# Layer 3's edge sweep: four groups' logits in one go, the scatter in two column halves, the leaky relu split between ScalarE and VectorE

## Chip, cores, metric

The kernel runs on 1 core of a Trainium2 chip. A time is the device time of one execution in microseconds (us). Names of engines: PE is TensorE, DVE VectorE, ACT ScalarE, POOL GpSimd, SP SyncE.

## What is computed

A chain of four graph layers over 6250 nodes and 100,000 edges (sorted by destination, padded to 106,496), features of 128 numbers, all in fp32, each layer with a residual and a layer norm ahead. The change touches the third, a GATv2 attention layer with H = 8 heads of O = 16:

```python
xl = (x @ W_l + b_l).reshape(-1, H, O)
xr = (x @ W_r + b_r).reshape(-1, H, O)
ee = (edge_attr @ W_e).reshape(-1, H, O)
m = jax.nn.leaky_relu(xl[src] + xr[dst] + ee, 0.2)
logits = jnp.einsum('eho,ho->eh', m, att)
lmax = jax.ops.segment_max(logits, dst, num_segments=N)
exl = jnp.exp(logits - lmax[dst])
denom = jax.ops.segment_sum(exl, dst, num_segments=N)
msg = xl[src] * (exl / (denom[dst] + 1e-16))[:, :, None]
out = jax.ops.segment_sum(msg, dst, num_segments=N).reshape(-1, H * O) + b_att
h = layer_norm(x + out)
h = layer_norm(h + gelu(h @ W1 + b1) @ W2 + b2)
```

Layers 1 and 2 are a sum and a mean over edges, layer 4 two smaller attention convolutions.

## The kernel before

The program is a row of phases: setup, `term_sweep` (layer 1), `norm1_phase`, `sum_sweep` (layer 2), `soft_sweep(2)` (layer 3), `ffn_phase`, `soft_sweep(3)` and `soft_sweep(4)` (layer 4). A sweep goes over G = 208 groups of GE = 512 edges, four tiles of 128 edges (TPG) each. Four consecutive groups are a batch (BATCH = 4).

Every engine has its own hand-written program, a function `step(t)` that is called for t = 0 to G + 7; what an engine does for group g in step t is set by `t.back(k)`, that is g = t - k. `sweep16` unrolls 16 steps into one turn of a loop. Engines meet only at semaphores, and each runs its own list in order. `wait_past(eng, sem, g, n, add)` waits for n * g + add counts.

`soft_sweep(2)`, called soft2 below, with lines of the kernel before:

- GpSimd gathers the 512 source rows of a group, four indirect DMAs (L1792), into one of 16 slots of `rows`; a slot is free when `message` of 16 groups earlier is done.
- TensorE, step t: `edge_terms(t)` transposes the four row tiles (L1867) and computes W_e times edge attributes plus destination rows times one-hot columns (L1873, L1874) into one PSUM bank, `term_bank`. `scatter(t-7)` (L1908) multiplies a one-hot (128 edges x 64 nodes of a window) with the message (128 edges x 136: 128 features and 8 weights), four tiles into one bank. `head_logits(t-1)` (L1881) multiplies `att8[:, j]` with `z`; each of a batch's four groups adds its 8 heads into its own rows of 32 lanes. `flip_window(t-7)` (L1930, L1931) transposes the window.
- Once in four steps: the carry matmul (L1956), the init matmul (L1940), four lane transposes (L1963) and the factor matmuls (L1969, L1970).
- ScalarE: copy of the transposed rows into `z` (L1829), the message's weight columns (L1824), the window (L1834), per batch the lanes (L1850), exponentials (L1838, L1840) and weights (L1818).
- VectorE: the leaky relu of t-1 in place in `z` (L2075), the addition of window t-8 into the sums in SBUF (L2009 to L2018), the message t-7 (L2066), the edge sum (L2094); per batch two scans over 512 columns for the running maximum (L2028, L2034), the carry (L2041, L2044), the shift of the lanes (L2050 to L2060) and the factors (L2080, L2081).
- SyncE issues the loads: attributes, one-hot columns, destination rows, one-hots (L1765, which waits for the scatter three groups earlier), and per batch `starts` and `cont`, the masks of the scans.

## Time and profile before

| | us |
|---|---|
| median of 3 runs | 7552.22 |
| lowest, highest | 7548.44, 7554.60 |
| span of the profiled execution | 5796.6 |
| median less span | 1755.6 |
| soft2, first to last start of TensorE's row transposes | 2290.1 to 3371.0 |

The profiled execution's own time was not kept. The span goes from the first to the last instruction in the profile; the runs' times are longer by a part that no row shows. An engine's busy time in a stretch is the sum of its instructions there without overlaps; matmuls are pipelined, so the length of one is longer than its share of the engine: the distance from one start to the next tells what it costs. A row of the timeline merges equal neighbours (x4), and behind it, in brackets, stands how long the engine was idle before it and what ended that.

### The profile page before, as it was taken

Reading aid. Unit: us, or ns where it says so; the run is one execution under the profiler, and the core shown is the slowest. Engines: PE = TensorE matmul, PEld = TensorE weight load, DVE = VectorE, ACT = ScalarE, POOL = GpSimd, SP = SyncE. Lnnn points to the kernel's source line nnn. Section 1 sums busy time; section 2 is a strip of 40 time slices with the busy share of each in tenths; the row PEclk is TensorE's granted clock in tenths of the full one; section 3 lists DMA queues with packets and bytes.
Section 4 is the critical chain, followed back from the end, with each engine's and each line's share of the span. In section 5 each row is a group of like instructions: output and inputs, shape, how many; then the busy total and the mean of one; then the engine's idle time right before and its main releaser. Section 6 shows DMA issues by size and latency. Waiting matters only on the chain. (4 is left out here: it accounts for less than half of the span.)

```text
span 5796.6 us, 89863 instructions
## 1 busy us (share of the span) xinstructions
PE 4596.1 (79%) x21959; PEld 3153.3 (54%) x21959; DVE 2702.8 (47%) x8105; ACT 1216.6 (21%) x3182; POOL 3988.9 (69%) x4207
## 2 busy tenths in 40 slices
PE   5888888657777776999999977687777758887887
PEld 4777777535556564444444433455555535555555
DVE  4222222321111113677777766555555545555555
ACT  2111111221211211222222258111111111111111
POOL 6777777457777775777777700777777747777775
PEclk9999999975555555999999989666666666666665
DMA  5333333244444443555555510455555534444443
GB/s 151 106 105 105 105 104 104 74 150 106 112 114 107 118 114 90 160 165 165 165 165 164 166 38 24 109 114 114 113 114 115 113 77 107 111 109 110 109 111 78
DMA packets 559823, 663.58 MB, mean 114 GB/s; under 512 B 196431, under 2 KB 390909, under 8 KB 558717
## 3 DMA queue, kind: packets, MB, share of 16 engines
q1 hardware_dynamic: 424909, 382.99, 22.2%
q0 software_dynamic: 134640, 277.80, 21.1%
q14 instruction: 207, 1.70, 0.1%
q8 instruction: 67, 1.10, 0.1%
HBM read 580.95 MB, written 86.19 MB: 115 GB/s over the span
## 5 line engine op out<-in xcount | busy, mean ns | idle before, releaser
L1792 POOL DMA_INDIRECT soft_rows<-table,sources x2496 | 2388.6, 957 | 1128.2 <-issue 737.7
L1422 POOL DMA_INDIRECT sum_rows<-table,sources x832 | 785.7, 944 | 343.9 <-issue 249.6
L1088 POOL DMA_INDIRECT term_rows<-table,sources x832 | 791.4, 951 | 289.4 <-issue 289.4
L1923 PE MATMUL psum<-soft_onehot,soft_message 128*128 128x64 f32 x3328 | 647.6, 358 | 107.1 <-DVE soft_message L2066 105.0
L1923 PEld LDWEIGHTS psum<-soft_onehot,soft_message 128*128 128x128 f32 x3328 | 586.1, 266 | 188.0 <-issue 181.8
L1119 PE MATMUL psum<-term_onehot,term_term 128*128 128x64 f32 x1664 | 403.9, 425 | 188.5 <-DVE sums L1171 176.6
L1464 PE MATMUL psum<-sum_onehot,sum_rows 128*128 128x64 f32 x1664 | 360.4, 391 | 222.7 <-DMA sum_rows<-table,sources 218.4
L1119 PEld LDWEIGHTS psum<-term_onehot,term_term 128*128 128x128 f32 x1664 | 370.7, 328 | 242.1 <-issue 242.0
L1165 DVE TENSOR_TENSOR term_term<-psum,term_rows 128x512 f32<-128x512 f32 x208 | 143.9, 692 | 753.0 <-issue 349.0
L1464 PEld LDWEIGHTS psum<-sum_onehot,sum_rows 128*128 128x128 f32 x1664 | 343.5, 304 | 278.0 <-issue 273.8
L1919 PEld LDWEIGHTS psum<-soft_onehot,soft_weights 128*4 128x4 f32 (+1 forms) x3328 | 284.9, 109 | 305.9 <-issue 293.0
L1109 PE MATMUL psum<-L_We,term_attrs 64*128 64x128 f32 x1664 | 430.5, 438 | 8.4 <-DMA term_attrs<-in_ea64T 8.4
L2066 DVE TENSOR_TENSOR soft_message<-soft_rows,psum 128x512 f32<-128x512 f32 x624 | 418.0, 670 | 2.9 <-issue 2.9
L1892 PE MATMUL psum<-soft_onehotT,soft_dst_cols 128*16 128x512 f32 (+1 forms) x416 | 375.4, 1004 | 49.4 <-DMA soft_dst_cols<-adst 49.4
L1109 PEld LDWEIGHTS psum<-L_We,term_attrs 64*128 64x128 f32 x1664 | 370.0, 325 | 56.4 <-issue 28.6
L1919 PE MATMUL psum<-soft_onehot,soft_weights 128*4 128x64 f32 (+1 forms) x3328 | 358.5, 272 | 12.4 <-DVE weight_sums L2011 0.9
L1097 ACT ACTIVATE term_term<-term_term 128x512 f32<-128x512 f32 x208 | 130.9, 630 | 913.0 <-DVE term_term L1165 913.0
L2016 DVE TENSOR_TENSOR sums<-sums,psum 128x64 f32 x624 | 136.7, 219 | 380.3 <-PE psum L1923 320.5
L1898 PE MATMUL psum<-ident,soft_src_cols 128*16 128x128 f32 (+1 forms) x832 | 173.5, 379 | 175.9 <-ACT soft_src_cols L1806 174.5
L1441 ACT ACTIVATE sum_flat<-psum 64x512 f32<-64x512 f32 x208 | 122.7, 590 | 830.9 <-PE psum L1454 826.4
L1503 DVE TENSOR_TENSOR sums<-sums,psum 128x64 f32 x208 | 46.2, 222 | 530.0 <-PE psum L1465 526.8
L1908 PEld LDWEIGHTS psum<-soft_message,soft_onehot 128*64 128x64 f32 x1664 | 188.1, 139 | 139.6 <-issue 138.8
(277 smaller groups left out, 6619.9 us busy)
## 6 DMA issues: line engine op xcount, KB each, us to landing
soft_onehotT<-onehotsT SPq DMA_DIRECT2D x312, 256.0 KB
soft_onehot<-onehots SPq DMA_DIRECT2D x624, 128.0 KB, 2.1
soft_attrs<-in_ea128T SPq DMA_DIRECT2D x208, 256.0 KB
soft_rows<-table,sources POOLq DMA_INDIRECT x2496
term_attrs<-in_ea64T SPq DMA_DIRECT2D x208, 128.0 KB, 2.8
onehots<-term_onehot SPq DMA_DIRECT2D x208, 128.0 KB
sum_onehot<-onehots SPq DMA_DIRECT2D x208, 128.0 KB, 2.7
onehotsT<-sum_flat SPq DMA_DIRECT2D x208, 128.0 KB
```

The source lines that it names most:

```text
L1088: pool.indirect_dma_start(rows[:, k, t, :], None, io.table0[0:NCH * CN], bass.IndirectOffsetOnAxis(sb.sources[:, g * TPG + t:g * TPG + t + ...
L1109: last = pe.matmul(term_bank[g.slot(4)][:, piece(b)], attrs[:, g.slot(AHEAD), piece(b)], sb.L0_We, start=True, stop=True)
L1119: last = pe.matmul(window[q], term[:, g.slot(4), b, :], onehot[:, g.slot(8), b], start=b == 0, stop=b == TPG - 1)
L1422: pool.indirect_dma_start(rows[:, k, t, :], None, io.table1[0:NCH * CN], bass.IndirectOffsetOnAxis(sb.sources[:, g * TPG + t:g * TPG + t + ...
L1464: pe.matmul(window[q], rows[:, g.slot(AROUND), b, 0:D], onehot[:, k, b], start=b == 0, stop=b == TPG - 1)
L1792: pool.indirect_dma_start(rows[:, k, t, :], None, table[0:NCH * CN], bass.IndirectOffsetOnAxis(sb.sources[:, g * TPG + t:g * TPG + t + 1], ...
L1892: pe.matmul(lane_bank[g.half()], dst_cols[:, j // 2], onehotT[:, pair(g)], start=j == 1, stop=False).then_inc(s.edge_term, 2)
L1898: last = pe.matmul(lane_bank[g.half()][:, piece(b)], src_cols[:, b], sb.ident, start=False, stop=b == TPG - 1)
L1908: last = pe.matmul(window_bank, onehot[:, k, b], message[:, g.slot(2), b, :], start=b == 0, stop=b == TPG - 1)
L1919: pe.matmul(bank[0:H, P:P + W], weights[:, q, b, j::BATCH], onehot[:, k, b], start=b == 0, stop=b == TPG - 1)
L1923: last = pe.matmul(bank[:, 0:W], message[:, g.slot(4), b, :], onehot[:, k, b], start=b == 0, stop=b == TPG - 1)
L2066: v.tensor_tensor(message[:, g.slot(2 if full else 4), :, 0:D].rearrange("p t (h c) -> p t h c", h=H), rows[:, g.slot(AROUND), :, 0:D].rea ...
```

## The change

soft2 gets a function of its own, `gatv2_sweep`; soft3 and soft4 keep `soft_sweep`, from which its branches for layer 3 are cut.

- **Logits.** `z` has four slots instead of two. `head_logits` runs once in four steps, for the whole batch, four groups back: four matmuls, each with the same `att_cols` (128 x 32, of which 8 columns hold the attention vector) and its own slot of `z`, into partitions 0 to 31, 32 to 63, 64 to 95 and 96 to 127 of `lane_bank`. Lanes, `starts` and `cont` so have 128 partitions, 32 a group with 8 in use; there is one `lane_bank`, and SyncE loads `starts` and `cont` in four pieces each.
- **Scatter.** Tiles 0 and 2 add into partitions 0 to 63 of the window bank, tiles 1 and 3 into 64 to 127. The window is copied with 128 partitions, and `flip_window` follows the scatter at once; it multiplies with `fold` (two 64 x 64 identities, one over the other), which turns the window and adds the halves.
- **Leaky relu.** VectorE adds the transposed rows, which ScalarE copied to `raw`, in place in PSUM (`term_bank`, now two banks). ScalarE writes a fifth of that into `z`. VectorE takes the maximum of both.
- The lane transposes become matmuls with `quad_pick`, which leaves out the empty lanes; the other small operands are laid out for 128 partitions. On VectorE the window's addition comes ahead of the leaky relu, and the backward scan behind the edge sum. `onehotT` has two slots of two groups instead of four.

```diff
-                    wait_past(pe, s.z, g, 1, 0)
+                    wait_past(pe, s.leaky, g, 1, -1)
...
                 def head_logits(g):
-                    j = g.slot(BATCH)
-                    pe.wait_ge(s.leaky, g.times(1, 1))
-                    if j == 0 and g.back(2 * BATCH).exists():
-                        pe.wait_ge(s.shifted, g.back(2 * BATCH).uses(BATCH))
-                    pe.matmul(lane_bank[g.half()], sb.att8[:, j], z[:, g.slot(2)], start=j == 0, stop=j == BATCH - 1).then_inc(s.logits, 1)
+                    pe.wait_ge(s.leaky, g.times(1, BATCH))
+                    if g.back(BATCH).exists():
+                        pe.wait_ge(s.factor_log, g.back(BATCH).uses(BATCH))
+                    settle(pe)
+                    for j in range(BATCH):
+                        last = pe.matmul(lane_bank[j * QUAD:(j + 1) * QUAD], sb.att_cols, z[:, j], start=True, stop=True)
+                    last.then_inc(s.logits, 1)
...
                     for b in range(TPG):
-                        last = pe.matmul(window_bank, onehot[:, k, b], message[:, g.slot(2), b, :], start=b == 0, stop=b == TPG - 1)
+                        last = pe.matmul(window_bank[b % 2 * W:b % 2 * W + W], onehot[:, k, b], message[:, g.slot(2), b, :], start=b < 2, stop=b >= TPG - 2)
...
                 def flip_window(g):
                     pe.wait_ge(s.window_copied, g.times(1, 1))
                     wait_past(pe, s.order, g, ORDER, 0)
                     settle(pe)
-                    pe.transpose(window_T[0][:, 0:W], window[:, 0:D], sb.ident[0:W, 0:W])
-                    pe.transpose(window_T[0][0:H, P:P + W], window[:, D:D + H], sb.ident[0:W, 0:W]).then_inc(s.window_T, 1)
+                    pe.matmul(window_T[:, 0:W], window[:, 0:D], fold, start=True, stop=True)
+                    pe.matmul(window_T[0:H, P:P + W], window[:, D:D + H], fold, start=True, stop=True).then_inc(s.window_T, 1)
...
-                            last = pe.transpose(weights_bank[:, b * L:(b + 1) * L], lanes[:, piece(b)], sb.ident[0:L, 0:L])
+                            last = pe.matmul(weights_bank[:, b * L:(b + 1) * L], lanes[:, piece(b)], sb.quad_pick, start=True, stop=True)
...
+                        act.activation(z[:, g.slot(BATCH)], term_bank[g.slot(2)], ACT.Copy, scale=0.2).then_inc(s.fifth, 1)
...
-                        act.activation(z[:, g.slot(2)], rows_bank, ACT.Copy).then_inc(s.rows_out, 1)
+                        act.activation(raw[:, g.slot(2)], rows_bank, ACT.Copy).then_inc(s.rows_out, 1)
...
-                        v.scalar_tensor_tensor(z[:, g.slot(2)], z[:, g.slot(2)], 0.2, z[:, g.slot(2)], ALU.mult, ALU.max).then_inc(s.leaky, 1)
+                    v.tensor_tensor(z[:, g.slot(BATCH)], term_bank[g.slot(2)], z[:, g.slot(BATCH)], ALU.max).then_inc(s.leaky, 1)
...
-                        v.tensor_tensor(z[:, g.slot(2)], term_bank, z[:, g.slot(2)], ALU.add).then_inc(s.z, 1)
+                    v.tensor_tensor(term_bank[g.slot(2)], term_bank[g.slot(2)], raw[:, g.slot(2)], ALU.add).then_inc(s.z, 1)
```

TensorE, the step that holds the init and lane matmuls, before (`psum<-` names what a matmul reads, then the output's shape):

```order
L1867 MATMUL psum<-ident,soft_rows 128x128 x4
L1873 MATMUL psum<-soft_attrs,L_We 128x512
L1874 MATMUL psum<-soft_onehotT,soft_dst_rows 128x512
L1940 MATMUL psum<-ones,soft_shift 32x1
L1908 MATMUL psum<-soft_message,soft_onehot 64x136 x4
L1881 MATMUL psum<-soft_z,att 32x512
L225 REGISTER_ALU
L1930 MATMUL psum<-ident,soft_window 128x64
L1931 MATMUL psum<-ident,soft_window 8x64
L1963 MATMUL psum<-ident,soft_lanes 128x32 x4
```

and now, the same step:

```order
L1827 MATMUL psum<-ident,soft_rows 128x128 x4
L1833 MATMUL psum<-soft_attrs,L_We 128x512
L1834 MATMUL psum<-soft_onehotT,rel_group 128x512
L1871 MATMUL psum<-ones,soft_shift 128x1
L1852 MATMUL psum<-soft_message,soft_onehot 64x136 x4
L225 REGISTER_ALU
L1859 MATMUL psum<-soft_fold,soft_window 128x64
L1860 MATMUL psum<-soft_fold,soft_window 8x64
L1889 MATMUL psum<-quad_pick,soft_lanes 128x32 x4
```

The logits are gone from between scatter and flip. They stand ahead of the scatter in one step of four:

```order
L1833 MATMUL psum<-soft_attrs,L_We 128x512
L1834 MATMUL psum<-soft_onehotT,rel_group 128x512
L1842 MATMUL psum<-soft_z,att_cols 32x512 x4
L1852 MATMUL psum<-soft_message,soft_onehot 64x136 x4
L225 REGISTER_ALU
L1859 MATMUL psum<-soft_fold,soft_window 128x64
```

There four matmuls run in a row where each step had one. VectorE, the step with the forward scan, before, from the window's addition on:

```order
L2018 TENSOR_TENSOR weight_sums<-weight_sums,psum 8x64
L2066 TENSOR_TENSOR soft_message<-soft_rows,psum 128x4x128
L2023 REGISTER_ALU
L2027 REGISTER_ALU
L2028 SCALAR_TENSOR_TENSOR psum<-soft_starts,psum 32x512
L2032 TENSOR_SCALAR soft_fend<-lane_mask,psum 32x4
L2034 SCALAR_TENSOR_TENSOR psum<-soft_starts,psum 32x512
L2092 REGISTER_ALU
L2094 TENSOR_TENSOR soft_z<-psum,soft_z 128x512
```

and now:

```order
L1938 TENSOR_TENSOR weight_sums<-weight_sums,psum 8x64
L1990 TENSOR_TENSOR soft_z<-psum,soft_z 128x512
L1983 TENSOR_TENSOR soft_message<-soft_rows,psum 128x4x128
L1942 REGISTER_ALU
L1943 REGISTER_ALU
L1944 SCALAR_TENSOR_TENSOR psum<-soft_starts,psum 128x512
L1948 TENSOR_SCALAR soft_fend<-quad_mask,psum 128x4
L1993 REGISTER_ALU
L1995 TENSOR_TENSOR psum<-psum,soft_raw 128x512
L1952 SCALAR_TENSOR_TENSOR psum<-soft_starts,psum 128x512
```

The leaky relu (L1990, the maximum) has come between the addition and the message, and the edge sum (L1995) ahead of the backward scan (L1952).

## Rows read from the trace of the kernel before

**Rows 1.** The page: span and instructions.

```profile
span 5796.6 us, 89863 instructions
```

**Rows 2.** Busy time by stretch: stretch, us, each engine, clock, DMA share, GB/s.

```profile
0.00:28.00 28.00, 5.55 (x20) 3.58 (x20) 14.11 (x81) 13.38 (x35) 23.24 (x47) 1.00 0.94 275
2320.00:2330.00 10.00, 8.48 (x24) 3.31 (x22) 3.81 (x9) 4.03 (x8) 7.56 (x9) 0.67 0.40 117
2371.00:3327.00 956.00, 933.82 (x4214) 437.03 (x4214) 690.39 (x1785) 278.55 (x776) 729.27 (x744) 1.00 0.56 165
3385.00:3407.00 22.00, 13.24 (x58) 9.85 (x56) 6.81 (x29) 3.26 (x13) 0.00 (x0) 0.50 0.02 6
```

**Rows 3.** Groups of soft2, 2300 to 3390: busy, mean ns | idle before, releasers.

```profile
L1792 POOL DMA_INDIRECT soft_rows<-table,sources x818 | 801.3, 980 | 249.4 <-issue 245.5 <-DVE soft_message L2066 4.0
...
L2075 DVE SCALAR_TENSOR_TENSOR soft_z<-soft_z 128x512 f32<-128x512 f32 x207 | 142.3, 688 | 31.8 <-issue 26.9
...
L1829 ACT ACTIVATE soft_z<-psum 128x512 f32<-128x512 f32 x206 | 123.0, 597 | 193.7 <-PE psum L1867 188.2
...
L2034 DVE TENSOR_TENSOR_SCAN psum<-soft_starts,psum 32x512 f32<-32x512 f32 x52 | 63.3, 1217 | 1.8
```

**Rows 4.** The gathers of soft3, 3700 to 4500, from the same view.

```profile
L1792 POOL DMA_INDIRECT soft_rows<-table,sources x641 | 605.5, 945 | 195.4 <-issue 191.7 <-DVE soft_message L2066 3.7
```

**Rows 5.** Line 1867, the row transposes: durations, first and last start.

```profile
L1867 PE MATMUL psum<-ident,soft_rows x832: 272/273/477, 2290.1 to 3371.0; 128*128 128x128 f32 x167
```

**Rows 6.** Timeline of TensorE over four steps: start, us, what.

```profile
2896.38 0.65 PE L1867 MATMUL psum<-ident,soft_rows 128*128 128x128 f32 x4
2896.87 1.02 PE L1873 MATMUL psum<-soft_attrs,L_We 128*128 128x512 f32 x2
2897.83 1.12 PE L1874 MATMUL psum<-soft_onehotT,soft_dst_rows 64*128 64x512 f32 x2
2898.88 1.14 PE L1908 MATMUL psum<-soft_message,soft_onehot 128*64 128x136 f32 x8
2899.95 1.05 PE L1881 MATMUL psum<-soft_z,att 128*32 128x512 f32 x2
2900.93 0.27 PE L1930 MATMUL psum<-ident,soft_window 64*128 64x64 f32 x1
...
2901.18 0.66 PE L1867 MATMUL psum<-ident,soft_rows 128*128 128x128 f32 x4
...
2911.31 0.40 PE L1963 MATMUL psum<-ident,soft_lanes 32*128 32x32 f32 x4 [0.17 <-ACT soft_lanes L1838]
2911.73 0.35 PE L1969 MATMUL psum<-soft_factors,lane_expand 32*128 32x4 f32 x2
2912.01 0.19 PE L1970 MATMUL psum<-soft_factors,lane_head 32*8 32x4 f32 x2
...
2916.94 0.33 PE L1867 MATMUL psum<-ident,soft_rows 128*128 128x128 f32 x1
```

**Rows 7.** Timeline of the drain of soft2: window copy, flip.

```profile
3381.27 0.28 ACT L1834 ACTIVATE soft_window<-psum 64x136 f32<-64x136 f32 x1 [1.76 <-PE psum L1908]
...
3381.69 0.24 PE L1930 MATMUL psum<-ident,soft_window 64*128 64x64 f32 x1 [0.46 <-ACT soft_window L1834]
```

**Rows 8.** Timeline of VectorE: the shift of the lanes.

```profile
2909.05 0.74 DVE L2055 SCALAR_TENSOR_TENSOR psum<-soft_cont,soft_init,psum 32x512 f32<-32x512 f32 x1
2909.83 0.68 DVE L2057 TENSOR_TENSOR soft_lanes<-soft_lanes,psum 32x512 f32<-32x512 f32 x1
```

**Rows 9.** Timeline: a leaky relu, the gather inside it, the next addition.

```profile
2894.91 0.69 DVE L2075 SCALAR_TENSOR_TENSOR soft_z<-soft_z 128x512 f32<-128x512 f32 x1
2895.02 1.40 POOL L1792 DMA_INDIRECT soft_rows<-table,sources  x1 [0.30 <-issue]
...
2896.28 0.21 DVE L2009 TENSOR_SCALAR sums<-sums,soft_factor_of  x1 [0.68 <-issue]
```

**Rows 10.** SyncE's waits in soft2: us in total, times, longest.

```profile
SPq L1765 <- PE psum L1908: 521.1, 203, 6.2
```

More of the change, by code:

```diff
@@ L1659, in soft_sweep @@
+    spread = {3: sb.lane_expand4, 4: sb.ones}[layer]
     mask, heads = sb.lane_mask[0:L], sb.lane_head[0:L, 0:H]
     AHEAD = 4
-    DST = AHEAD if full else BATCH
     phase = f"soft{layer}"
-    FIRST = AROUND if full else 4 * AROUND
-    LAST = G + LAG if full else STEPS * (NCH - 1 + BEHIND) + 14
-    names = ("order cleared starts_in cont_in rows_T rows_out edge_term z leaky src_out logits lanes_out running backward fend carry_psum carry shift init_psum init maxima "
-             "shifted factor_log weights_lane factor spread weights_T weights_out factor_psum factor_out columns message "
-             "scattered window_copied window_T").split()
@@ L1668, in soft_sweep @@
-    s = sems(nc, phase, *names, gathered=AROUND, attr=AHEAD, dst_rows=DST, onehotT=4, onehot=4)
+    FIRST = 4 * AROUND
+    LAST = STEPS * (NCH - 1 + BEHIND) + 14
+    names = ("order cleared starts_in cont_in edge_term leaky src_out logits lanes_out running backward fend carry_psum carry shift init_psum init maxima "
+             "shifted factor_log weights_lane factor spread weights_T weights_out factor_psum factor_out message "
+             "scattered").split()
+    s = sems(nc, phase, *names, gathered=AROUND, dst_rows=BATCH, onehotT=4, onehot=4)
@@ L1676, in soft_sweep @@
         onehotT = tile("onehotT", [2 * W, 4, GE])
-        message = tile("message", [P, 2, TPG, D + H] if full else [P, 4, TPG, D])
+        message = tile("message", [P, 4, TPG, D])
         starts = tile("starts", [L, GE + 1])
@@ L1711, in soft_sweep @@
         factor_head_bank = sb.psum[0:H, 7, 48:48 + BATCH]
-        nodes = None if full else GatNodes(nc, io, sb, tile, layer, sb.psum[:, 2, :])
-        CLEARED = 4 + (not full)
+        nodes = GatNodes(nc, io, sb, tile, layer, sb.psum[:, 2, :])
+        CLEARED = 5
         ORDER = 4
@@ L1809, in step @@
                 def step(t):
-                    if not full and t.back(BATCH).closes(0):
+                    if t.back(BATCH).closes(0):
                         take_sources(t.back(BATCH))
@@ L1846, in step @@
                     if g.closes(0):
-                        act.wait_ge(s.logits, g.times(1, BATCH) if full else g.uses(BATCH))
+                        act.wait_ge(s.logits, g.uses(BATCH))
                         if g.back(BATCH).exists():
@@ L1899, in src_logits @@
                     last.then_inc(s.logits, 1)
-                def scatter(g):
-                    k = g.slot(4)
-                    wait_past(pe, s.window_copied, g, 1, 0)
-                    pe.wait_ge(s.onehot[k], g.uses(4, 16))
-                    pe.wait_ge(s.columns, g.times(1, 1))
-                    pe.wait_ge(s.message, g.times(1, 1))
-                    for b in range(TPG):
-                        last = pe.matmul(window_bank, onehot[:, k, b], message[:, g.slot(2), b, :], start=b == 0, stop=b == TPG - 1)
-                    last.then_inc(s.scattered, 1)
                 def scatter_T(g):
@@ L1942, in step @@
                     if g.exists():
-                        (scatter if full else scatter_T)(g)
-                    if full and t.back(1).exists():
-                        head_logits(t.back(1))
-                    if not full and t.back(BATCH).closes(0):
+                        scatter_T(g)
+                    if t.back(BATCH).closes(0):
                         src_logits(t.back(BATCH))
-                    if g.exists() and full:
-                        flip_window(g)
                     g = t.back(BATCH + 1)
@@ L2021, in running_max @@
                     n = g.uses(BATCH)
[L2022 removed]
+                    logits, highest = lane_bank[g.half()], running_bank
                     v.wait_ge(s.lanes_out, n)
[L2024 to L2026 removed]
+                    v.scalar_tensor_tensor(logits, logits, 0.2, lanes, ALU.mult, ALU.max).then_inc(s.leaky, 1)
+                    v.wait_ge(s.leaky, n)
                     v.wait_ge(s.starts_in, g.uses(BATCH, 16))
@@ L2071, in step @@
                 def step(t):
-                    g = t.back(1)
-                    if g.exists() and full:
-                        v.wait_ge(s.z, g.times(1, 1))
-                        v.scalar_tensor_tensor(z[:, g.slot(2)], z[:, g.slot(2)], 0.2, z[:, g.slot(2)], ALU.mult, ALU.max).then_inc(s.leaky, 1)
                     g = t.back(LAG)
@@ L2843, in laid_out @@
     group_last = dst[GE - 1::GE]
-    lane = np.arange(8 * BATCH)
+    lane = np.arange(4 * BATCH)
+    quad, slot = np.arange(P) // QUAD, np.arange(P) % QUAD
     return {
```

474 lines of the change are left out of this document (367 added, 107 removed).

## The prediction, made before the changed kernel ran

> **What bounds the kernel now.** I read the page first: span 5796.6 us [rows 1]. The runs' median is 7552.2 us, so 1755.6 us lie outside the span; no time of the profiled execution's own is given. I leave that part as it is and add the change of the span to the median. The diff touches one stretch, layer 3's edge sweep (soft2), and small things around it; soft3 and soft4 keep their instructions. A measurement of this kernel can tell about 0.2% (15 us) from no change.
>
> Next the stretch itself. From 2371 to 3327 us TensorE is busy 933.8 of 956 us at a granted clock of 1.00 (2.4 GHz), VectorE 690, GpSimd 729 [rows 2]. GpSimd's gathers sit there back to back: 801.3 us busy and 249.4 us between them for 818, so 1.285 us each, 5.14 us for a group's four; the 0.3 us between two is issue [rows 3]. In soft3 the same line takes (605.5 + 195.4) / 641 = 1.249 us each, 5.00 us a group [rows 4]. TensorE's first row transposes start at 2290.1 and 3371.0 us, 207 groups apart: 5.22 us a group [rows 5]. So TensorE is the slower of two engines that run within 2% of each other, and the step that matters is TensorE's. A gain on it can't bring the group under the gathers' 5.00 us: at most 208 x 0.22 = 46 us.
>
> TensorE's step, start to start [rows 6]: transposes 0.49, the attribute matmul 0.96, the destination matmul 1.05, scatter 1.07, logits 0.98, window flip 0.25: 4.80 us. Four steps take 20.56 (2896.38 to 2916.94), 1.35 more than 4 x 4.80 for the carry, init, lane and factor matmuls. 16 x 5.22 leaves 1.3 us for each turn of the loop of 16 steps.
>
> **The change part by part, on TensorE.**
> - Logits. Before, 4 x 0.98 = 3.92 us in four steps. A matmul is two passes (x2) of 0.43 us (0.86 for two, and about 0.1 until the next shape starts). After, four matmuls stand together, each into its own 32 columns. No row shows neighbours in different column strips. One bound is no overlap: 8 x 0.43 + 0.10 = 3.54. The other is that both passes of all four overlap: 2 x 0.43 + 0.10 = 0.96. I take 5 passes: the two of one matmul use the same strip and follow one another, as the eight of the scatter do in 1.07 us; if starts stay in program order, only the second pass of one can lie beside the first of the next. 5 x 0.43 + 0.10 = 2.25.
> - Scatter, same reasoning on its two halves: 8, 5 or 4 passes of 0.12: 1.07, 0.67, 0.55. I take 0.67.
> - Flip. Two transposes, 0.25, become two matmuls against fold, each in two passes: between 0.25 and 0.50; 0.40, near the two 128-column passes of L1969 (0.28 from 2911.73 to 2912.01) with a small one behind.
> - Lane transposes, 0.42 (2911.31 to 2911.73), become matmuls of two passes: 0.42 to 0.86; I take 0.86, since the pass and not the row count is what L1963 pays for. Factors, carry and init stay (0.40, 0.12, 0.15).
>
> Own work in four steps: 4 x (0.50 + 2.01 + 0.67 + 0.40) + 2.25 + 0.12 + 0.15 + 0.86 + 0.40 = 18.1 us, against 20.3 now. That alone would put TensorE at 4.5 us and the gathers in front.
>
> **What the change adds is waits.** The logits stood between scatter and flip and hid ScalarE's copy of the window. In the drain, where no logits stand there, the row shows the cost: the copy L1834 starts at 3381.27, takes 0.28, and the flip L1930 starts at 3381.69 after 0.46 idle, 0.53 with the tail of the last pass [rows 7]. After, every step pays it: 4 x 0.53 = 2.1 us. I then walked a batch through the new order with the same durations (VectorE's 0.67 to 0.69 us passes, 1.22 a scan, ScalarE's 0.60, about 0.1 us from one engine to the next) [rows 3, 6, 8]. The scans are now of 128 partitions, at the same 512 columns; I keep 1.22. Zero is the start of a step with logits:
> - Step A: transposes and edge matmuls to 2.51, logits to 4.76, scatter to 5.43, flip 5.96 to 6.36. No other wait: the fifth and the maximum of the group before were done.
> - Step B: edge matmuls to 8.87, scatter to 9.54, flip to 10.48, carry to 10.60. VectorE does the maximum, the message, the forward scan (8.33 to 9.57), the sum, and at 10.52 the backward scan.
> - Step C: edge matmuls to 13.11, init to 13.26. VectorE leaves the backward scan at 11.7, has carry and shift to 12.25, the window's addition to 12.78, the maximum to 13.42, the message to 14.09: scatter starts at 14.23, **0.97 late**. Flip to 15.84. The exponential waits for the shifted lanes (0.74 and 0.68 us) and ends at 16.35: lane matmuls at 16.49, **0.65 late**, factors to 17.75.
> - Step D: edge matmuls to 20.26. VectorE copies the factors, loads the window columns (0.68 us of issue before L2009), adds, takes the maximum and weighs until 20.66: scatter at 20.80, **0.54 late**. Flip to 22.41.
>
> That is 18.1 + 2.1 + 2.2 = 22.4 us; with a quarter of the loop turn (0.33) 22.7, or 5.68 us a group. The same walk on the old order gives 20.7 without the loop turn, where the trace has 20.56 [rows 6]. Sum: 208 x (5.68 - 5.22) = **+96 us**; the drain adds about 1 us (four logits at once). The span would be 5894.
>
> **On other engines.** ScalarE gets one more copy, 208 x 0.60 = 125 us, at 279 busy of 956 now; it lies beside TensorE except where the walk has it. VectorE trades L2075 (0.69) for a pass of like length. L2075 reads only SBUF; gather 2895.02, inside it, takes 1.40 us where others take 0.94 [rows 9], and this is what stands between 1.285 and 1.249. After, the maximum has one operand in PSUM, so gathers should fall to 1.25. It is worth nothing while TensorE needs 5.68: GpSimd runs ahead until its 16 slots are full and waits for messages. The Trainium skill says the same in "SBUF — State Buffer", "Who interferes with whom": a VectorE instruction with two SBUF inputs contends with a GpSimd instruction that reads SBUF, one with a single SBUF input does not. By that rule alone the sweep would win 208 x 4 x 0.036 = 30 us, but only with TensorE below 5.0.
>
> SyncE issues starts and cont in four pieces each, 6 more issues in four steps; now it waits 521 us in the sweep for L1908 [rows 10], and the pieces stand behind no new wait that ends late: onehotT's two slots ask for edge terms three steps old, which the scatter wait ahead of it already implies. Nothing for it. The setup loads three more constants: GpSimd has 47 instructions in 23.2 us there, so at most 1.5 us [rows 2].
>
> **Rivals.**
> 1. Strips don't overlap. Logits 3.54, scatter 1.07: the walk gives 6.18 us a group (the longer logits hide some waits), +200: 7752 us. For it: no row shows two strips at once.
> 2. Strips overlap fully: 0.96 and 0.55 give 18.1 - 1.29 - 0.48 = 16.3 of own work, but the waits grow to 4.5: 5.30 a group, +17: 7570 us; with cheap flips and lane matmuls 5.17, 7542. The Trainium skill, "TensorE: Matmul & The Clock Gate", Part 3, reports three 32-column matmuls side by side at 2.38x; by that figure the four logits come nearer to this case than to mine. No row here bears on it.
> 3. Faster: the gathers set the pace. It decides where TensorE's four steps, waits included, fall under 20.0 us, that is 2.7 below my walk: full overlap, cheap flips, and VectorE's message no longer late. Then 5.00 us: -47, 7505 us.
> 4. The clock falls. TensorE now idles in short pieces, 4.3 of 22.7 us. It stood at 0.67 from 2320 to 2330, with busy 8.5 of 10, and at 0.50 (1.2 GHz) in the drain, busy 13 of 22 [rows 2]. If it is 0.9 in the mean, 18.1 us of own work take 2.0 more: another 104 us, 7753 us. Against it: most gaps are 0.5 us.
>
> **How the numbers follow.** Forecast 7649 us: 0.43 (7610 to 7690). Rival 1: 0.20; rival 2: 0.12; rival 3: 0.10; rival 4: 0.12; worse than all, 0.03. Faster by over 0.2%: rival 3 and a little of 2, 0.12. Within: most of the rest of 2, 0.07. Slower: 0.81. The range, 7540 to 7790, leaves out rival 3 and what lies above 7790.
>
> **What would show it.** Start to start of the row transposes: 5.7 us, by fours about 6.4, 4.2, 7.2, 4.7. Idle before the flip, put down to ScalarE's window copy, in nearly all 208 steps. Scatter waiting for the message in two of four steps. Eight logit passes in about 2.2 us. Gathers at 0.945 us, with waits for the message. It is wrong if the transposes come every 5.0 us with gathers ending the wait, if the window copy shows no idle, or if the granted clock in the sweep is below 1.00.

## The result, and the profile after

The changed kernel takes 7716.21 us in the median of three runs (7692.23 to 7736.21), the kernel before 7552.22: a ratio of 1.0209, with a 95% interval from 1.0188 to 1.0231. The forecast was 7649 us, 7540 to 7790, slower with 0.81. The sign and the range held. The way there did not, and the experiments show two reasons.

The first is about the measurement. In these runs both kernels take about 30% longer than the profile of before shows. Later, on three chips, the kernel before took 5800 to 5803 us, which is the 5796.6 us span of [rows 1] and some 2 us around it. So the 1755.6 us that the prediction put outside the span are not a fixed part: the page of before came from an execution of another speed than the runs beside it. Every time below is therefore compared with the kernel before on the same chip. On one of the three the change costs more, not less: 6059.94 us against 5800.35, 1.0448 (1.0430 to 1.0465). That is where its cause is looked for here. At the speed of the recorded runs the kernel before has no trace, so what makes up their 164 us is not shown.

The page of the changed kernel in the recorded runs: span, busy time, and the clock and TensorE in 40 slices.

```profile
span 7690.5 us, 92103 instructions
PE 4925.6 (64%) x22583; PEld 3387.3 (44%) x22583; DVE 2685.6 (35%) x8104; ACT 1311.9 (17%) x3390; POOL 3960.4 (51%) x4210
PE   2667667455556656888778876466666646666666
PEclk9999999855555556676666678566565656566566
```

The same page on one of the three chips (run a1_after, the same program):

```profile
span 6045.3 us, 92103 instructions
PE 4720.4 (78%) x22583; PEld 3237.0 (54%) x22583; DVE 2687.4 (44%) x8104; ACT 1319.3 (22%) x3390; POOL 3960.7 (66%) x4210
PE   5888888577777777888888887577877767788777
PEclk9999999996555556777877778766667666666666
```

VectorE, ScalarE and GpSimd are busy for the same time on both chips, within 1% (2686, 1312, 3960 us). TensorE is busy 205 us longer on the first, and all engines wait more. The part of the program to look at is layer 3's sweep, in slices 16 to 24 of the second page. The transposes of the rows tell how long it lasts, as line 1867 did in [rows 5]. Line 1827 is that line after. One line's instructions (durations, first and last start), after, in the recorded runs:

```profile
L1827 PE MATMUL psum<-ident,soft_rows x832: 272/417/477, 2834.3 to 4512.7; 128*128 128x128 f32 x167
```

The same of a1_after:

```profile
L1827 PE MATMUL psum<-ident,soft_rows x832: 272/327/477, 2285.7 to 3614.6; 128*128 128x128 f32 x167
```

And line 1867 of the kernel before, profiled again (b1_before):

```profile
L1867 PE MATMUL psum<-ident,soft_rows x832: 272/273/476, 2289.8 to 3375.7; 128*128 128x128 f32 x167
```

A group takes 8.1 us, 6.4 us, and 5.2 us before. The sweep on the other chip is 243 us longer than before (1328.2 against 1085.5 from the first to the last group's start), and the whole span 242 us (6045.3 against 5803.7), so next to nothing is won or lost elsewhere. The median duration of one transpose already hints at the cause: 273 ns before, 327 after, with the same minimum of 272.

Busy time in the same stretch as the third line of [rows 2] (engines PE, PEld, DVE, ACT, POOL, then the granted clock, DMA share, GB/s), of a1_after:

```profile
2371.00:3327.00 956.00, 841.21 (x3887) 414.20 (x3886) 554.64 (x1461) 301.35 (x783) 575.95 (x612) 0.78 0.48 135
```

Of b1_before, in two halves:

```profile
2371.00:2871.00 500.00, 488.60 (x2200) 228.24 (x2200) 359.75 (x932) 146.17 (x407) 381.32 (x390) 1.00 0.56 165
2871.00:3327.00 456.00, 444.41 (x2009) 208.23 (x2010) 328.54 (x850) 133.61 (x372) 347.76 (x356) 1.00 0.56 165
```

The granted clock is 0.78 where it was 1.00. It toggles between its two levels, 1.2 and 2.4 GHz. Two batches of four steps in a1_after show what that does, in the same view: one at full clock, the other with much of it at the lower level.

```profile
2675.70:2696.40 20.70, 17.74 (x106) 9.12 (x105) 14.44 (x38) 8.22 (x21) 15.27 (x17) 1.00 0.59 168
2623.20:2651.50 28.30, 25.40 (x105) 11.70 (x104) 14.97 (x39) 7.94 (x21) 14.85 (x17) 0.68 0.44 118
```

The work is the same (106 and 105 matmul records), VectorE and ScalarE take what they took, and TensorE's 17.7 us become 25.4. By the starts of line 1827, of the 34 batches of groups 16 to 199 that lie clear of the loop's turn, 6 run at full clock and take 20.65 us in the mean, and 14 have a mean clock under 0.70 and take 28.3 us. Before, all 34 run at full clock and take 20.56 us. So **at full clock a batch of the new sweep is as fast as one of the old (20.65 against 20.56 us), and nearly all that the sweep loses, it loses to the clock.**

The batch at full clock, TensorE's timeline, to be laid beside [rows 6]:

```profile
2675.66 0.65 PE L1827 MATMUL psum<-ident,soft_rows 128*128 128x128 f32 x4
2676.15 1.02 PE L1833 MATMUL psum<-soft_attrs,L_We 128*128 128x512 f32 x2
2677.10 1.12 PE L1834 MATMUL psum<-soft_onehotT,rel_group 64*128 64x512 f32 x2
2678.15 1.06 PE L1842 MATMUL psum<-soft_z,att_cols 128*32 128x512 f32 x8
2679.15 0.68 PE L1852 MATMUL psum<-soft_message,soft_onehot 128*64 128x136 f32 x8
2680.40 0.41 PE L1859 MATMUL psum<-soft_fold,soft_window 128*128 128x64 f32 x2 [0.57 <-ACT soft_window L1799]
2680.74 0.28 PE L1860 MATMUL psum<-soft_fold,soft_window 128*8 128x64 f32 x2
2680.95 0.66 PE L1827 MATMUL psum<-ident,soft_rows 128*128 128x128 f32 x4
...
2685.28 0.66 PE L1827 MATMUL psum<-ident,soft_rows 128*128 128x128 f32 x4
...
2687.77 0.38 PE L1871 MATMUL psum<-ones,soft_shift 8*128 8x1 f32 x2
2688.18 0.68 PE L1852 MATMUL psum<-soft_message,soft_onehot 128*64 128x136 f32 x8
...
2690.67 1.05 PE L1889 MATMUL psum<-quad_pick,soft_lanes 128*128 128x32 f32 x8 [0.63 <-ACT soft_lanes L1809]
...
2691.98 0.66 PE L1827 MATMUL psum<-ident,soft_rows 128*128 128x128 f32 x4
...
2694.48 0.68 PE L1852 MATMUL psum<-soft_message,soft_onehot 128*64 128x136 f32 x8
```

Four logits, eight passes, take 1.06 us; one took 1.05 in [rows 6]. The column strips overlap completely. The scatter takes 0.68 us in place of 1.14. The window copy stands open before each flip. All of TensorE's waits over the stretch of 956 us (a1_after; us in total, times, longest):

```profile
PE psum L1859 <- ACT soft_window L1799: 82.7, 150, 0.7
PE psum L1889 <- ACT soft_lanes L1809: 22.8, 37, 0.7
PE psum L1842 <- DVE soft_z L1990: 6.6, 4, 1.8
PE psum L1852 <- DVE soft_message L1983: 0.3, 1, 0.3
```

Together they come to 112 of 956 us. All but the four before the logits, at turns of the loop, are 0.7 us or less.

When does the clock fall? In this stretch it falls 27 times, and all these falls begin at the same place: from 0.7 us before to 2.3 us after the start of the lane matmuls (L1889). There two waits stand close together, one for the window copy and one for the exponential. The timeline before the fall at 2713.7 us (a1_after), and busy time on either side of it:

```profile
2711.88 0.41 PE L1859 MATMUL psum<-soft_fold,soft_window 128*128 128x64 f32 x2 [0.59 <-ACT soft_window L1799]
...
2713.01 1.24 PE L1889 MATMUL psum<-quad_pick,soft_lanes 128*128 128x32 f32 x8 [0.52 <-ACT soft_lanes L1809]
```

```profile
2693.20:2713.70 20.50, 15.96 (x94) 7.88 (x93) 13.58 (x33) 7.07 (x19) 13.80 (x16) 1.00 0.54 153
2713.70:2734.20 20.50, 19.46 (x63) 8.77 (x63) 8.32 (x24) 4.72 (x13) 10.14 (x11) 0.50 0.38 105
```

At the lower clock TensorE is busy nearly all the time for much less work (63 matmul records against 94). So its busy share in a mixed stretch is no measure of how much it has to do.

### The profile page after: what moved, and what is told of

The parts are those of the page before. It is cut to its first block and busy times, and to the rows that moved or that the text cites. A ratio compares the mean times of both kernels' runs of the same rounds, so it can differ in the third digit from the quotient of the medians.

```text
span 7690.5 us, 92103 instructions
## 1 busy us (share of the span) xinstructions
PE 4925.6 (64%) x22583; PEld 3387.3 (44%) x22583; DVE 2685.6 (35%) x8104; ACT 1311.9 (17%) x3390; POOL 3960.4 (51%) x4210
## 5 line engine op out<-in xcount | busy, mean ns | idle before, releaser
L2145 POOL DMA_INDIRECT soft_rows<-table,sources x1664 | 1571.1, 944 | 1586.5 <-DVE soft_message L2353 726.8
L1769 POOL DMA_INDIRECT soft_rows<-table,sources x832 | 784.7, 943 | 936.6 <-DVE soft_message L1983 624.1
L2226 PE MATMUL psum<-soft_onehot,soft_message 128*128 128x64 f32 x3328 | 697.0, 378 | 516.7 <-DVE soft_message L2353 494.0
L2226 PEld LDWEIGHTS psum<-soft_onehot,soft_message 128*128 128x128 f32 x3328 | 633.0, 284 | 604.0 <-issue 596.8
L2222 PEld LDWEIGHTS psum<-soft_onehot,soft_weights 128*4 128x4 f32 (+1 forms) x3328 | 303.4, 113 | 309.8 <-issue 297.3
L2222 PE MATMUL psum<-soft_onehot,soft_weights 128*4 128x64 f32 (+1 forms) x3328 | 383.6, 285 | 17.3 <-ACT soft_weights L2171 3.5
L2305 DVE TENSOR_TENSOR sums<-sums,psum 128x64 f32 x416 | 91.8, 221 | 802.2 <-DMA soft_onehot<-onehots 316.5
L1834 PE MATMUL psum<-soft_onehotT,rel_group 64*128 64x512 f32 x416 | 332.5, 891 | 0.0
L1503 DVE TENSOR_TENSOR sums<-sums,psum 128x64 f32 x208 | 46.1, 222 | 803.1 <-remote 654.9
L1833 PE MATMUL psum<-soft_attrs,L_We 128*128 128x512 f32 x416 | 323.9, 873 | 0.0
```

The source lines that it names most:

```text
L1769: pool.indirect_dma_start(rows[:, k, t, :], None, io.table2[0:NCH * CN], bass.IndirectOffsetOnAxis(sb.sources[:, g * TPG + t:g * TPG + t + ...
L1833: pe.matmul(term_bank[g.slot(2)], sb.L2_We, attrs[:, k], start=True, stop=False)
L1834: pe.matmul(term_bank[g.slot(2)], dst_rows[side(g), k], onehotT[side(g), pair(g)], start=False, stop=True).then_inc(s.edge_term, 1)
L2145: pool.indirect_dma_start(rows[:, k, t, :], None, table[0:NCH * CN], bass.IndirectOffsetOnAxis(sb.sources[:, g * TPG + t:g * TPG + t + 1], ...
L2222: pe.matmul(bank[0:H, P:P + W], weights[:, q, b, j::BATCH], onehot[:, k, b], start=b == 0, stop=b == TPG - 1)
L2226: last = pe.matmul(bank[:, 0:W], message[:, g.slot(4), b, :], onehot[:, k, b], start=b == 0, stop=b == TPG - 1)
```

## The experiments

Twelve kernels ran. "Stretch" is always 2371 to 3327 us of layer 3's sweep.

**The kernel before, once more.**

> The kernel before, unchanged, profiled once more. It asks whether the page of before (span 5796.6 us against a median of 7552 us) shows what the timed runs do. In the profile of after every sweep is longer than on that page, the untouched ones too (soft3 1386 us against 1040). Theory 1 (the page of before came from a quieter execution): the span comes out near 7550 us, soft3 near 1380 us, and the sweep of layer 3 at 1400 to 1550 us, with late wakes at TensorE's semaphores. Theory 2 (a fixed 1755 us lie outside the span, and the change itself slows the other sweeps): the span is again near 5800 us and soft3 near 1040.

5806.23 us (span 5803.7), soft3 from first to last gather 1039 us, layer 3's sweep as on the page of before. The span is theory 2's, but the 1755 us outside it are not there, and theory 1's long sweeps aren't either: what differs is the speed of the runs beside that page. The seven plain runs of before in this group took 5799 to 5806 us.

**The kernel after, unchanged, on such a chip.** It is the base of all that follows.

> The kernel after, unchanged, where the kernel before takes 5803 us (if this chip is again such a one). With the fill of 0.5 us in each step the kernel took 5830 us at a clock of 0.96 in layer 3's sweep. Theory 1 (TensorE's idle lets the clock fall, and the fill holds it): without the fill the mean clock in the sweep is 0.7 to 0.8 and the time 6030 to 6120 us, 1.04 to 1.055 of before, although there is less to do. Theory 2 (the fill only filled idle time, the clock is a matter of the chip): the sweep is as with the fill, 5800 to 5840 us, clock 0.96.

6059.94 us, 1.0448; clock 0.78 in the stretch. Theory 1: without the fill of the next run the clock is low and the time 230 us longer.

**Four idle transposes in the gap.** 4 x 0.12 us of TensorE work that nobody reads, where it waits for the copy:

```
-                    pe.wait_ge(s.window_copied, g.times(1, 1))
                     wait_past(pe, s.order, g, ORDER, 0)
                     settle(pe)
+                    for b in range(TPG):
+                        pe.transpose(window_T[:, 256:256 + P], sb.ident, sb.ident)
+                    pe.wait_ge(s.window_copied, g.times(1, 1))
+                    settle(pe)
```

> The kernel after, with four 128x128 transposes of the identity into an unused part of the flip's bank, between scatter and flip: 0.5 us of TensorE work for nothing in each of 208 steps, inside the idle that waits for the window's copy. Theory 1 (the granted clock falls because TensorE idles there): the mean clock in layer 3's sweep rises from 0.68 towards 0.9, and the sweep gets shorter by 100 us or more although it has more to do. Theory 2 (the clock has another cause): clock 0.65 to 0.70 as in after; time within 0 to +60 us of after's 7716, since at the lower clock the fill takes up to 1 us of a 0.6 us gap.

5829.66 us, 1.0048 (1.0032 to 1.0065). Busy time in its stretch:

```profile
2371.00:3327.00 956.00, 907.18 (x5318) 498.06 (x5318) 653.50 (x1730) 359.16 (x929) 691.49 (x733) 0.96 0.56 160
```

Clock 0.96 in place of 0.78, and 230 us fewer than a1_after (two chips, each against its own before: 1.0448 and 1.0048), by adding work. This is the experiment that decides between waits and clock. Its four steps take 5.20, 4.24, 6.70 and 4.20 us at full clock, together 20.34 where a1_after has 20.65 at full clock: 0.3 us in each of 52 batches, some 16 of the 230 us, is not the clock's doing. The clock still falls 14 times: 6 times at the lane matmuls, and 8 times at a turn of the loop, where TensorE waits 1.5 to 2.0 us before the logits.

**Half of it** (`range(2)` in place of `range(TPG)`).

> The kernel after with two transposes of the identity in place of four between scatter and flip: half the fill, 0.25 us in the idle of each step. None gave 1.0448 of before with a clock of 0.78 in the sweep's stretch, four gave 1.0048 with 0.96. Theory 1 (TensorE's activity sets the clock, step by step): between the two, clock 0.83 to 0.92, ratio 1.015 to 1.035. Theory 2 (what matters is that no idle of 0.5 us is left): near the full fill, 1.005 to 1.01.

5909.42 us, 1.0187 (1.0170 to 1.0204), clock 0.88. Its stretch, same view:

```profile
2371.00:3327.00 956.00, 895.17 (x4618) 460.18 (x4617) 607.50 (x1610) 334.74 (x867) 642.46 (x682) 0.88 0.53 149
```

None, two and four transposes give 0.78, 0.88 and 0.96, and 1.045, 1.019 and 1.005 of before: a dose and its effect.

**The same four behind the flip, where TensorE doesn't wait.**

```
+                        for b in range(TPG):
+                            last = pe.transpose(window_T[:, 256:256 + P], sb.ident, sb.ident)
+                        last.then_inc(s.window_T, 1)
```

> The kernel after with the four transposes of the identity behind the flip, where TensorE does not wait, so that the idle before the flip stays: the same work as in the fill, on the path. Theory 1 (the amount of TensorE work in a stretch sets the clock, not where the idle lies): the clock rises to 0.9 or more; at full clock a batch is 20.5 + 4 x 0.5 = 22.5 us less what its other idle takes up, 5.3 to 5.6 us a group, so 5840 to 5920 us in all, faster than after unchanged (6060) although everything added is on the path. Theory 2 (the idle before the flip itself is what lowers it): clock 0.75 to 0.8, and slower than after, 6090 to 6170.

5987.45 us, 1.0321 (1.0303 to 1.0338), clock 0.90. Its stretch:

```profile
2371.00:3327.00 956.00, 855.84 (x4654) 459.35 (x4653) 575.62 (x1512) 314.16 (x814) 604.67 (x643) 0.90 0.50 140
```

At full clock its batch takes 22.08 us against 20.65, so 1.4 us of the added 2 lie on the path, and the kernel is still 1.2% faster than without them. The idle before the flip is all there; the wait for the exponential is gone, since the four transposes stand ahead of the lane matmuls and cover it. The clock still falls 25 times, 24 of them within 3.2 us of a flip that waited alone, but it stays low for 8 us each time (0.10 x 2 x 956 / 25), where a1_after has 15. Theory 1 had the direction and the clock; its 5840 to 5920 us were too hopeful, since 0.90 is not 1.00.

**The flip behind the next step's row transposes**, so that useful work covers the copy.

```
                     if t.exists():
-                        edge_terms(t)
+                        row_transposes(t)
+                    if t.back(LAG + 1).exists():
+                        flip_window(t.back(LAG + 1))
+                    if t.exists():
+                        edge_terms(t)
```

> The kernel after, with the window flip of a group moved behind the row transposes of the next step, so that 0.5 us of TensorE work lies beside ScalarE's copy of the window. Theory 1 (the exposed copy is what the change costs): the 0.47 to 0.64 us of idle before the flip goes, 4 x 0.5 = 2 us in four steps or more at the lower clock, 208 x 0.5 = 105 us, so about 7610 us (0.986 of after, 1.008 of before). Theory 2 (late messages and late wakes set the step, the copy is hidden behind them): the idle moves to the scatter, within 20 us of after's 7716.

6048.1 us, 1.0419 (1.0402 to 1.0437). Busy time in its stretch:

```profile
2371.00:3327.00 956.00, 869.02 (x3864) 435.57 (x3860) 549.28 (x1450) 291.48 (x781) 578.01 (x613) 0.76 0.47 134
```

The 82.7 us of waits before the flip are gone from the list of waits, and 0.3% of the time with them, where theory 1 wanted 1.4%. Most of the idle only moved: to the exponential (59.4 us before the lane matmuls, 22.8 in a1_after), to the carry matmul (16.9 us) and to the scatter (8.4 us), 85 us in all where a1_after has 112. The clock is 0.76. It falls 37 times in the stretch, each time within 0.9 us before to 2.5 us after the start of the lane matmuls, whose wait is two and a half times as long as in a1_after:

```profile
2714.34 1.05 PE L1894 MATMUL psum<-quad_pick,soft_lanes 128*128 128x32 f32 x8 [1.56 <-ACT soft_lanes L1809]
```

The work that was moved covers the waits before the flip and leaves one long wait at the lane matmuls.

**The scatter in one piece.** Undone: the column halves and the fold (eight passes in a row, a flip by transposes).

```
-  window_bank[b % 2 * W:b % 2 * W + W], onehot[:, k, b], ..., start=b < 2, stop=b >= TPG - 2
+  window_bank, onehot[:, k, b], ..., start=b == 0, stop=b == TPG - 1
```

> The kernel after with one part undone: the scatter in one piece of 64 columns (eight passes in a row, 1.07 us in place of 0.58) and the window flipped by transposes. 0.5 us more TensorE work in each step, as in the fill, but on the path. Theory 1 (the clock rewards TensorE work whether useful or not): the clock is above that of after unchanged by 0.05 or more, and the time is below it by 30 us or more. Theory 2 (a faster scatter is worth what it saves): slower than after unchanged by 208 x 0.3 to 0.5 = 60 to 100 us.

6122.82 us, 1.0548 (1.0529 to 1.0566), 63 us over a1_after, as theory 2 said. Its stretch:

```profile
2371.00:3327.00 956.00, 856.78 (x3363) 457.69 (x3362) 520.57 (x1367) 281.46 (x737) 545.08 (x578) 0.75 0.45 127
```

So the column halves are worth having within this kernel. TensorE has more to do in each step here and the clock is lower, 0.75. "More work, higher clock" is therefore not the whole rule. Where the work stands matters: the undone scatter leaves both waits open at the lane matmuls, and all 35 falls of the clock in its stretch begin there. The fill covers the first of the two. What exactly the chip goes by, these runs don't settle.

**The leaky relu in one VectorE pass over SBUF**, with ScalarE writing no fifth.

```
-  v.tensor_tensor(z[:, g.slot(BATCH)], term_bank[g.slot(2)], z[:, g.slot(BATCH)], ALU.max)
+  v.scalar_tensor_tensor(z[:, g.slot(BATCH)], z[:, g.slot(BATCH)], 0.2, z[:, g.slot(BATCH)], ALU.mult, ALU.max)
```

> The kernel after with one part undone: the leaky relu is again one VectorE pass over two SBUF operands, and ScalarE writes no fifth. TensorE's order is after's. Theory 1 (the split only matters for the gathers, and these are not the bound): within 20 us of after unchanged, with gathers of 1.3 to 1.4 us again where they meet that pass. Theory 2 (the two-step relu delays z, which the four logits wait for, by 0.6 us once in four steps): 52 x 0.6 = 31 us faster than after unchanged.

6074.3 us, 1.0477 (1.0458 to 1.0497), 14 us over a1_after and hardly apart from it. The gathers of the stretch by groups (busy, mean ns | idle before, releasers), a1_after:

```profile
L1769 POOL DMA_INDIRECT soft_rows<-table,sources x612 | 577.4, 943 | 380.4 <-DVE soft_message L1983 228.8 <-issue 151.5
```

leaky_old:

```profile
L1769 POOL DMA_INDIRECT soft_rows<-table,sources x604 | 581.6, 963 | 376.1 <-DVE soft_message L1983 223.7 <-issue 152.4
```

b1_before:

```profile
L1792 POOL DMA_INDIRECT soft_rows<-table,sources x745 | 729.4, 979 | 227.1 <-issue 224.4 <-DVE soft_message L2066 2.7
```

943, 963, 979 ns. The split relu frees the gathers of their slow cases, as forecast, and it is worth nothing, or too little to tell, while GpSimd waits for messages.

**The logits one group per step again**, each into its own 32 rows, with two lane banks; the small outputs move into the flip's bank.

```
-                    for j in range(BATCH):
-                        last = pe.matmul(lane_bank[j * QUAD:(j + 1) * QUAD], sb.att_cols, z[:, j], start=True, stop=True)
+                    pe.matmul(lane_banks[g.half()][j * QUAD:(j + 1) * QUAD], sb.att_cols, z[:, j], start=True, stop=True)
```

> The kernel after, with one part undone: the logits of a group are taken in the step behind it again, between scatter and flip, each into its own 32 rows of one of two banks, two passes each. Everything else is after's. Four steps: 3.9 us of logits in place of 1.0, and 2.1 us of exposed window copy gone. Theory 1 (side by side is nearly free, and what it costs is the uncovered copy and the idle that lowers the clock): the two cancel within 1 us of four steps, and the clock is that of before, so the time is 7550 to 7680 us. Theory 2 (the batch saves TensorE 2.9 us and the exposed copy is covered anyway): slower than after by 208 x 0.4 = 80 us or more, near 7800.

5826.56 us, 1.0043 (1.0026 to 1.0059). Busy time in its stretch:

```profile
2371.00:3327.00 956.00, 919.02 (x4632) 425.69 (x4632) 662.15 (x1739) 362.00 (x934) 698.09 (x741) 0.99 0.56 162
```

Theory 1. Undoing the one part that saves TensorE the most, 2.9 us in four steps, makes the kernel 4% faster. Clock 0.99; a batch at full clock takes 20.72 us, the same again. The logits cover the window copy. What is left are 14.4 us of waits before the lane matmuls and 21.2 us before 11 scatters, and the clock falls 6 times, behind waits of 1.6 to 2.6 us at turns of the loop.

**Two versions on top of the fill.** mid_fill has the logits between scatter and flip, the fill in the other three steps only, and VectorE's maximum ahead of its window additions; fill_first has the fill in every step and the same maximum first:

```
+                    if t.back(1).exists():
+                        leaky(t.back(1))
                     g = t.back(LAG)
                     if g.closes(0):
```

> A version meant to beat both: the kernel after with the four logits between scatter and flip (where they cover the window's copy), the fill of four transposes there in the other three steps, and VectorE's maximum for the leaky relu ahead of its window additions. With the fill alone a batch takes 20.3 us (steps 5.20, 4.24, 6.70, 4.20), and the first step of 16 takes 3.0 us more. If the theory holds (clock held at 0.96 or more by the fill, and the first step 0.5 us shorter), a batch takes 19.8 us and the gathers' 20.0 set the pace: the sweep ends near 1050 us, the whole at 5790 to 5805, within 0.3% of before. If the clock falls again because three steps only are filled: 5850 or more.

5856.15 us, 1.0086 (1.0064 to 1.0108), clock 0.91. The clock falls more often again, its last case. That the one fill left out does it is not shown, since the places of the logits and of the maximum changed too. At full clock a batch takes 20.4 us, and not the 19.8 hoped for.

> The fill of four transposes in every step, and VectorE's maximum for the leaky relu ahead of its factor copies and window additions, so that at the turn of the loop the four logits don't wait for VectorE's column loads (0.95 us) and additions. Other three steps of four as with the fill (4.24, 6.70, 4.20). Theory 1: first step of 16 shorter by 1 to 1.5 us, less clock loss behind it: 13 x 1.5 + a few = 20 to 30 us below the fill alone (5830), 5800 to 5810, no different from before. Theory 2 (the maximum ahead of the message makes messages later where they are late already): 52 x 0.7 x 2 = 70 us slower than the fill alone.

5833.78 us, 1.0067 (1.0047 to 1.0088), clock 0.97. It aimed at the turn of the loop, where the first of 16 steps takes 8.21 us with the fill (part of it at the lower clock, 0.79 in the mean) and a like step elsewhere 5.20. There (timeline of fill_gap) TensorE's logits wait for a maximum that stands behind VectorE's branch and column loads:

```profile
2633.04 1.12 PE L1834 MATMUL psum<-soft_onehotT,rel_group 64*128 64x512 f32 x2
2634.30 0.21 DVE L1933 TENSOR_SCALAR sums<-sums,soft_factor_of  x1 [3.72 <-issue]
2634.90 0.67 DVE L1993 TENSOR_TENSOR soft_z<-psum,soft_z 128x512 f32<-128x512 f32 x1
2635.81 1.94 PE L1842 MATMUL psum<-soft_z,att_cols 128*32 128x512 f32 x8 [1.65 <-DVE soft_z L1993]
```

The batches with a turn fell from about 23.6 to 21.3 us, as theory 1 had it. The step with the lane matmuls rose from 6.70 to 6.84, and the clock fell in other batches instead (0.94 in the mean of those behind the one with the turn, 0.98 with the fill alone): no difference in the whole.

**Two parts of the change in the kernel before**: column halves and split relu, the logits left where they were.

```
+  pe.matmul(window_bank[b % 2 * W:b % 2 * W + W], onehot[:, k, b], message[:, g.slot(2), b, :], start=b < 2, stop=b >= TPG - 2)
+  v.tensor_tensor(z[:, g.slot(2)], term_bank[g.slot(2)], z[:, g.slot(2)], ALU.max)
```

> A version meant to beat both: the kernel before with two parts of the change alone, the scatter in two column halves with its flip against fold, and the leaky relu as the maximum of the PSUM sum and ScalarE's fifth (term banks 0 and 7, the small outputs in bank 6). The logits stay one group per step, four heads' layout and lane transposes as before. TensorE saves 0.45 us on the scatter and pays 0.15 to 0.2 on the flip in each step: steps of 4.5 instead of 4.80, a batch 19.3 to 19.5 us instead of 20.56; gathers of 0.945 us with 0.305 between them need 20.0. Theory 1 (TensorE stays busy enough for its clock, the logits cover the copy): the sweep goes at the gathers' pace, first gather to last 1042 to 1052 us in place of 1066, the whole 0.996 to 0.998 of before. Theory 2 (even this saving lets the clock fall): clock below 0.95 in the sweep, and 1.003 or more.

7513.01 us against 7471.62, 1.0058 (1.0045 to 1.0072), clock 0.85 from 2900 to 4300. This run fell on a chip of the slow kind, so it doesn't say what the version does at 5800 us. The time is theory 2's. Its clock can't be laid to the two parts: the kernel before has no trace there, and over the whole program its runs show 0.72 to 0.75, and those of this version 0.72 to 0.74. No version beat the kernel before.

## Why the prediction was right in sign and range, and where it failed

- **The bound** was read rightly: TensorE before, at 5.22 us a group, with the gathers behind it. They never set the pace after (228.8 us of waiting for messages).
- **Logits, 2.25 us: failed.** The step "if starts stay in program order, only the second pass of one can lie beside the first of the next" is wrong. Four matmuls take 1.00 us, the bound of 0.96. The Trainium skill, "TensorE: Matmul & The Clock Gate", Part 3, gives 2.38x for three column tiles; here four give 4 x 0.98 / 1.00 = 3.9x.
- **Scatter, 0.67: too large.** Its row has 0.68, but with the tail of the last pass. The eight passes start in four pairs, 0.01 us apart within a pair and 0.11 to 0.17 from one pair to the next: full overlap, the bound of 0.55.
- **Flip, 0.40: too small.** 0.55 from 2680.40 to 2680.95, over the bound of 0.50. Init, taken as 0.15, costs 0.31, from its start to that of the scatter where no message is late. Lane matmuls, 0.86: 0.88.
- **Exposed copy, 4 x 0.53:** right, 0.47 to 0.57 in each step. **Exponential 0.65 late:** right, 0.63.
- **Messages 0.97 and 0.54 late: failed.** In step C the message does end last, but it costs 0.10 us: it ends at 2688.03, the scatter starts 0.15 later, and that is 0.41 behind the init and not 0.31. In step D it ends 0.33 us before the scatter starts and costs nothing. VectorE's timeline (a1_after) shows why:

```profile
2686.64 0.20 DVE L1938 TENSOR_TENSOR weight_sums<-weight_sums,psum 8x64 f32 x1
2686.77 0.67 DVE L1990 TENSOR_TENSOR soft_z<-psum,soft_z 128x512 f32<-128x512 f32 x1
2687.37 0.67 DVE L1983 TENSOR_TENSOR soft_message<-soft_rows,psum 128x512 f32<-128x512 f32 x1
```

Passes of 0.67 us start 0.60 apart; the walk set them end to end, and over the chain of a step this makes 0.7 us (the message ends 2.76 us into the step, and 3.49 in the walk).
- **Sum at full clock.** The walk gave steps of 6.36, 4.23, 7.15, 4.65, together 22.4; the trace has 5.29, 4.33, 6.70, 4.40, together 20.7. At a turn of the loop the first step takes 6.9 to 7.3 us at full clock, 1.8 us more than a plain one, where before has 1.3. So at full clock the change would have cost 208 x 0.02 us for the steps and about 13 x 0.5 us for the turns: 11 us, an estimate. Rival 2, forecast at +17, comes nearest to that. It had the overlap right and the total, but not its parts: 16.3 us of work and 4.5 of waits, where the batch has 17.7 busy and 3.0 idle.
- **The clock, taken as 1.00: failed,** and this is the step that carries the result. Rival 4 had the mechanism and 0.12; it held "most gaps are 0.5 us" against itself, and the clock fell with gaps of just that size, where two of them came together. It also priced it at a mean of 0.9 where 0.78 came. Of the 243 us that the sweep is longer in a1_after, some 11 would be there at full clock, and the rest, about 230, is the clock's. fill_gap, at 0.96, gives back 230 us of the whole.
- **The base: failed.** "I leave that part as it is and add the change of the span to the median" joined two speeds. On a chip of the profile's kind the cost is 260 us where +96 was forecast; in the recorded runs it is 164, and what that consists of is open. That 7649 lies near 7716 owes as much to a waiting time that did not come (1.7 us too much in each batch, 52 x 1.7 = 88 us) as to insight. Right by its number, the forecast had the cause wrong, and its hit is luck in large part.

## What to carry to other kernels

Before taking work off a TensorE that is busy all the time at full clock, ask what its granted clock will be afterwards: here 2.9 us less of work in 20.6 cost 4%, and idle transposes bought it back. Look for the place where two short waits come together: cover one of them, and don't merge them. Read the granted clock of a stretch beside its busy time, and compare one batch at full clock with one at the lower before blaming a wait. And check that a profile's span stands near the runs' time; where it doesn't, it is from another speed, not a fixed part outside.

## What the runs showed of the hardware that was not expected

**The same program took 30% longer on some chips.** Three took 5800 to 5803 us for the kernel before, one 7472, and the recorded runs, whose chip is not on record, 7552. Each chip was used at one time only, so it may be the chip or something that went with the time. On the slow kind TensorE's records can end long before anyone who waits for them goes on. The timeline of after in the recorded runs, one scatter and the two engines that wait for what TensorE did there:

```profile
3114.83 0.68 PE L1852 MATMUL psum<-soft_message,soft_onehot 128*64 128x136 f32 x8 [0.26 <-issue]
...
3118.17 0.16 DVE L1968 COPY soft_init<-psum 128x1 f32<-128x1 f32 x1 [3.48 <-remote]
...
3121.05 0.28 ACT L1799 ACTIVATE soft_window<-psum 128x136 f32<-128x136 f32 x1 [4.56 <-remote]
```

The scatter's record ends at 3115.5, and the copy that waits for it starts at 3121.05, while gathers go on at 0.94 us. Over 2900 to 4400 us line 1799 has 187.9 us of such waits in 32 places ("remote"); a1_after has none. In 36 of the 208 groups the copy starts more than 1 us after the scatter's last record, up to 5.8 us; in a1_after never more than 0.13. Since ends are modelled, TensorE may well have stood still inside the scatter. The granted clock doesn't show it (0.68 in that stretch), and why this happens stays open: no run here varied it.

**The clock fell with no long gap anywhere.** In a1_after no wait of the stretch is over 0.7 us but for four before the logits, 6.6 us in all, and the clock is 0.78. It fell behind two waits of 0.5 to 0.7 us with 0.6 us of work between them. The Trainium skill, "TensorE: Matmul & The Clock Gate", "A second HAM failure mode: psum-queue depth-cycling", describes for another kernel short idles between groups of matmuls that make the clock go back and forth. This trace agrees, though the idles here are waits for ScalarE.
